# Second layer's codes transposed by DMA, both biases as 32-row tiles on TensorE

## What is computed

```python
def bit_linear(x, w, b):
    scale_x = 127.0 / clip(max(abs(x), axis=-1), 1e-05)
    x_dq = clip(round(x * scale_x), -128, 127) / scale_x
    w_dq = clip(round(w / gamma_w), -1, 1) * gamma_w      # gamma_w = mean(abs(w))
    return einsum('bsd,hd->bsh', x_dq, w_dq) + b
gate = silu(bit_linear(x, gate_w, gate_b))
val = bit_linear(x, val_w, val_b)
return bit_linear(gate * val, out_w, out_b)
```

## Time and profile before

| | |
|---|---|
| median of three runs | 839.48 us |
| profiled execution: its own time | 841.52 us |
| profiled execution: from first to last instruction (span) | 839.7 us |
| mean granted clock of TensorE | 0.970 of full speed |
| busy: TensorE, VectorE, ScalarE, GpSimd | 750.2, 697.7, 534.0, 240.2 us |
| DMA, mean rate over the span | 61 GB/s |

### The profile page before, as it was taken

The page is one execution under the profiler, slowest core; times in us unless marked ns, Lnnn a source line. Parts: engine busy times, 40 slices in busy tenths (PEclk is TensorE's granted clock), DMA queues, the critical chain, the costliest instruction groups (busy, mean ns, idle before and its releaser), DMA issues.

```text
span 839.7 us, 14590 instructions
## 1 busy us (share of the span) xinstructions
PE 750.2 (89%) x4886; PEld 384.6 (46%) x4886; DVE 697.7 (83%) x1412; ACT 534.0 (64%) x693; POOL 240.2 (29%) x427
## 2 busy tenths in 40 slices
PE   4695658969999999999999999999999999999995
PEld 4442344434544454445444544454445444454442
DVE  6778876898889888888988988988888888779982
ACT  4447858767557755784578557855676556745563
POOL 4101003221333324232433333314422332223431
PEclk9898768999999999999999999999999999999998
DMA  8572345101030103011211121111111020001000
GB/s 275 192 261 64 130 165 170 26 14 39 2 95 10 42 26 77 17 37 37 56 37 37 37 52 42 37 37 42 51 37 37 17 52 26 26 2 51 13 26 26
DMA packets 51663, 50.90 MB, mean 61 GB/s; under 512 B 30877, under 2 KB 30877, under 8 KB 50857
## 3 DMA queue, kind: packets, MB, share of 16 engines
q1 hardware_dynamic: 51624, 50.42, 19.2%
HBM read 39.91 MB, written 10.50 MB: 60 GB/s over the span
## 4 chain that ended last, share of the span: by engine, by line
PE 45%; DVE 31%; issue 11%; ACT 10%; POOL 1%; DMA 1%; DVEq 0%; POOLq 0%; ACTq 0%
PE psum L1444 14%; PE psum L1399 13%; PE psum L1435 7%; DVE arena L988 4%; DVE psum L983 3%; ACT arena L749 2%; DVE arena L1088 2%; PE psum L1402 2%; PE psum L1427 2%; PE psum L1378 2%; DVE xmax L1060 1%; DVE arena L1096 1%; PE psum L1470 1%; DVE stats L1048 1%; DVE arena L922 1%
## 5 line engine op out<-in xcount | busy, mean ns | idle before, releaser
L1399 PE MATMUL psum<-ternary,xqT 128*128 128x512 f16 x1024 | 261.3, 379 | 2.8 <-DVE xqT L1009 2.6
L554 POOL TENSOR_TENSOR rstd<-var_e,minus_half 128x1 f32<-128x1 f32 x64 | 40.0, 625 | 406.5 <-DVE var_e L1028 263.9
L1399 PEld LDWEIGHTS psum<-ternary,xqT 128*128 128x128 f16 x1024 | 96.3, 98 | 108.3 <-DVE xqT L1009 3.5
L1435 PE MATMUL psum<-ternary,arena 128*128 128x512 f16 x512 | 128.0, 383 | 1.2 <-ACT arena L726 1.2
L693 ACT ACTIVATE arena<-psum,dequant 128x512 f32<-128x512 f32 x128 | 87.2, 682 | 43.2 <-PE psum L1402 42.8
L983 DVE SCALAR_TENSOR_TENSOR psum<-psum,dequant,valb_b 128x512 f32<-128x512 f32 x128 | 96.3, 752 | 20.2 <-PE psum L1399 19.7
L988 DVE TENSOR_TENSOR arena<-psum,arena 128x512 f32<-128x512 f32 x128 | 88.5, 692 | 20.8 <-ACT arena L693 17.1
L1444 PE MATMUL psum<-wo_hi,arena 128*128 128x512 f16 x256 | 84.4, 392 | 2.5 <-DVE arena L1096 1.9
L1444 PE MATMUL psum<-arena,wq_hi 128*128 128x512 f16 x256 | 77.5, 385 | 7.1 <-ACT arena L740 7.1
L726 ACT ACTIVATE arena<-psum,round_c 128x1024 f16<-128x1024 f16 x64 | 71.3, 1114 | 19.1 <-PE psum L1427 18.7
L701 ACT ACTIVATE arena<-arena,round_c,hscale 128x1024 f32<-128x1024 f32 x64 | 75.9, 1236 | 4.6 <-DVE hscale L1004 4.4
(11 more groups left out here) (181 smaller groups left out, 1348.7 us busy)
## 6 DMA issues: line engine op xcount, KB each, us to landing
arena<-in_x SPq DMA_DIRECT2D x64, 256.0 KB, 2.7
out<-arena SPq DMA_DIRECT2D x32, 256.0 KB, 2.0
arena<-in_L_ffn_gate_w SPq DMA_DIRECT2D x4, 1024.0 KB, 10.0
arena<-in_L_ffn_out_w SPq DMA_DIRECT2D x3, 1024.0 KB, 9.6
ternary<-in_L_ffn_val_w SPq DMA_DIRECT2D x2, 1024.0 KB, 10.2
kcur<-k_scratch SPq DMA_DIRECT2D x64, 32.0 KB, 2.2
ternary<-in_ctx SPq DMA_DIRECT2D x1, 1024.0 KB, 5.4
ternary<-in_L_xattn_Wk SPq DMA_DIRECT2D x1, 1024.0 KB, 8.0
```

What stands on the lines that cost most here:

```text
L1399: ins = M.matmul(ps[:], xqT[:, t % 2, k, :], w[:, k, cols], start=(k == 0), stop=(w is wv and k == KC - 1))
L1435: ins = M.matmul(psO[:], hidT[:, k, :], wo2[:, k, :], start=(k == 0), stop=(k == FC - 1))
```

## The change

The codes of the second layer no longer go through TensorE. Behind the two roundings, `quant` now has two casts: each half of the rounded tile goes, with the rounding constant taken off, into a float16 buffer `hid16`. SP's new `hidden_T` waits for each cast and issues a transposing DMA from that half of `hid16` to `hidT`. `down` waits for both DMAs of its tile. `hidden_transpose`, ScalarE's `hidden_T` and their waits go; a tile's casts wait until the DMAs of the tile before have landed, and the first DMA of a tile for the last down matmul of the tile before. In the first row SP waits once for the last weight transpose.

The value's bias joins the gate's on TensorE: rows 0 to 31 of `bias_parts`, `inv_cols` and `inv_rows` are for the gate, rows 32 to 63 for the value. Both biases are now the first matmuls of a chunk, each with 32 rows, ahead of the eight others; so the gate product's four matmuls now stand behind the wait for psV as well. `hidden` is one pass. `valb_b` and its load go; GpSimd and SP prepare two biases where there was one (six loads of parts instead of three).

```diff
-        bias_left = sb("bias_left", [P, FC])
-        bias_cut = sb("bias_cut", [P, PARTS, FC], BF16)
-        valb_b = sb("valb_b", [P, F])
-
-        unused_abs = valb_b[:, 0:F // 2].bitcast(F16)
+        bias_left = sb("bias_left", [P, 2, FC])
+        bias_cut = sb("bias_cut", [P, 2, PARTS, FC], BF16)
+        hid16 = sb("hid16", [P, F], F16)
+        unused_abs = hid16[:, :]
         unused_abs_last = room(11)[:, 2 * D:].bitcast(F16)
         inv_cols = sb("inv_cols", [P, 2, P], BF16)
         inv_rows = sb("inv_rows", [P, 2, P], BF16)
-        inv = sb("inv", [P, 2])
-        inv_deq = sb("inv_deq", [P, 1])
-        ones_p = sb("ones_p", [P, PARTS])
+        inv = sb("inv", [P, 2, 2])
+        inv_deq = sb("inv_deq", [P, 2])
+        ones_p = sb("ones_p", [P, 2 * PARTS])
...
+            def hidden_T(row, t):
+
+                last, u = ahead(row, t, -1)
+                wait_alone(sp, s_met_sp, o_done, last, u + 1)
+                for h in range(2):
+                    wait_alone(sp, s_met_sp, h16_ready, row, 2 * t + h + 1)
+                    sp.dma_start_transpose(hidT[:, h * FC // 2:(h + 1) * FC // 2, :],
+                                           hid16[:, h * F // 2:(h + 1) * F // 2]).then_inc(hidT_loaded.sem, 16)
+
             def body(b, prev, ffn, att, pre):
                 a, c = b + 1, b + 2
                 for t in range(NT):
                     if pre and (b is not FIRST or t >= 2):
                         normed_x(c, t)
+                    if ffn and not prev and t == 1:
+                        sp.wait_ge(s_wtr, 3 * W_GROUPS)
+                    if prev if t == 0 else ffn:
+                        hidden_T(*ahead(b, t, -1))
...
-                        sp.wait_ge(s_wabs, 3 * W_CHUNKS - 1)
-                        sp.dma_start(valb_b[:, :], bcast(val_b, F)).then_inc(s_vbias, 16)
...
-            sp.wait_ge(s_bst, 16)
-            for i in range(PARTS):
-                sp.dma_start(bias_parts[PARTS * i:PARTS * (i + 1), :],
-                             bias_dram[i:i + 1, :].to_broadcast([PARTS, F])).then_inc(s_brow, 16)
+            sp.wait_ge(s_bst, 16 * 2)
+            for g in range(2):
+                for i in range(PARTS):
+                    row = GROUP * g + PARTS * i
+                    sp.dma_start(bias_parts[row:row + PARTS, :],
+                                 bias_dram[g, i:i + 1, :].to_broadcast([PARTS, F])).then_inc(s_brow, 16)
...
-                whole, left = inv[:, 0:1], inv[:, 1:2]
-                G.tensor_scalar(whole, inv_deq[:], xr[:, t:t + 1], None, ALU.mult).then_inc(iv_ready.sem, 1)
+                whole, left = (inv[:, n, :].rearrange("p (g a) -> p g a", a=1) for n in range(2))
+                cols = inv_cols[:, t % 2, :].rearrange("p (g c) -> p g c", c=GROUP)
+                G.tensor_scalar(inv[:, 0, :], inv_deq[:], xr[:, t:t + 1], None, ALU.mult).then_inc(iv_ready.sem, 1)
                 wait(pool, iv_ready, row, t + 1)
                 for j in range(PARTS):
                     src = left if j else whole
-                    G.tensor_tensor(inv_cols[:, t % 2, j:PARTS * PARTS:PARTS], ones_p[:],
-                                    src.to_broadcast([P, PARTS]), ALU.mult).then_inc(iv_part.sem, 1)
+                    G.tensor_tensor(cols[:, 0:2, j:PARTS * PARTS:PARTS], ones_p[:].rearrange("p (g c) -> p g c", g=2),
+                                    src.to_broadcast([P, 2, PARTS]), ALU.mult).then_inc(iv_part.sem, 1)
...
-                    if n == 0:
-                        last, u = ahead(b, t, -2)
-                        wait(act, hid_tr, last, 2 * u + 2)
...
+                    last, u = ahead(row, t, -1)
+                    wait(act, hidT_loaded, last, 16 * 2 * (u + 1))
+                    for h in range(2):
+                        cols = slice(h * F // 2, (h + 1) * F // 2)
+                        wait(act, hq_ready, row, 2 * t + h + 1)
+                        A.activation(hid16[:, cols], gs[:, t % 2, cols], ACT.Identity,
+                                     bias=round_c[:, 2:3]).then_inc(h16_ready.sem, 1)
...
-                def hidden_T(row, t, h):
-                    wait(act, hid_tr, row, 2 * t + h + 1)
-                    A.activation(hidT[:, h * FC // 2:(h + 1) * FC // 2, :].rearrange("p k n -> p (k n)"),
-                                 half(psO), ACT.Identity, bias=round_c[:, 1:2]).then_inc(hidT_ready.sem, 1)
...
-                    if not prev and (t, n) == (0, 0):
-                        dve.wait_ge(s_vbias, 16)
-                    V.scalar_tensor_tensor(out=psV[n % 2], in0=psV[n % 2], scalar=dequant[:, t, 1:2],
-                                           in1=valb_b[:, n * CW:(n + 1) * CW],
-                                           op0=ALU.mult, op1=ALU.add).then_inc(vb_ready.sem, 1)
-                    wait(dve, vb_ready, b, NCH * t + n + 1)
                     wait(dve, silu_done, b, NCH * t + n + 1)
-                    V.tensor_tensor(part, psV[n % 2], part, ALU.mult).then_inc(hid_ready.sem, 1)
+                    V.scalar_tensor_tensor(out=part, in0=psV[n % 2], scalar=dequant[:, t, 1:2], in1=part,
+                                           op0=ALU.mult, op1=ALU.mult).then_inc(hid_ready.sem, 1)
...
-                    for ps, w, done, used in ((psG[i % 2], wg, g_done, silu_done),
-                                              (psV[i % 2], wv, v_done, hid_ready)):
+                            pe.wait_ge(s_brow, 16 * 2 * PARTS)
+                    for g, (ps, used) in enumerate(((psG[i % 2], silu_done), (psV[i % 2], hid_ready))):
                         if n > 2:
                             wait(pe, used, b, n - 2)
+                        rows_g = slice(GROUP * g, GROUP * (g + 1))
+                        M.matmul(ps[:], inv_rows[rows_g, t % 2, :], bias_parts[rows_g, cols], start=True, stop=False)
+                    for ps, w, done in ((psG[i % 2], wg, g_done), (psV[i % 2], wv, v_done)):
                         for k in range(KC):
-                            ins = M.matmul(ps[:], xqT[:, t % 2, k, :], w[:, k, cols], start=(k == 0),
-                                           stop=(w is wv and k == KC - 1))
-                        if w is wg:
-                            ins = M.matmul(ps[:], inv_rows[:, t % 2, :], bias_parts[:, cols],
-                                           start=False, stop=True)
+                            ins = M.matmul(ps[:], xqT[:, t % 2, k, :], w[:, k, cols], start=False,
+                                           stop=(k == KC - 1))
                         ins.then_inc(done.sem, 1)
...
-                def hidden_transpose(row, t, h):
-
-                    codes = low(gs[:, t % 2, :])
-                    wait(pe, hq_ready, row, 2 * t + h + 1)
-                    if h == 0:
+                def down(row, t, chunks):
+
+                    if 0 in chunks:
                         last, u = ahead(row, t, -1)
                         wait(pe, ys_ready, last, u + 1)
-                    else:
-                        wait(pe, hidT_ready, row, 2 * t + 1)
-                    for i in range(FC // 2):
-                        k = h * FC // 2 + i
-                        ins = M.transpose(half(psO)[:, i * P:(i + 1) * P], codes[:, k * P:(k + 1) * P], eye16[:])
-                    ins.then_inc(hid_tr.sem, 1)
-
-                def down(row, t, chunks):
-
-                    if 0 in chunks:
-                        wait(pe, hidT_ready, row, 2 * t + 2)
+                        wait(pe, hidT_loaded, row, 16 * 2 * (t + 1))
```

More of the change, by code:

```diff
@@ L484, in _ @@
                 sp.dma_start(dst, src).then_inc(s_tab, 16)
-            sp.dma_start(bias_left[:, :], gate_b.rearrange("(p c) -> p c", p=P)).then_inc(s_bias, 16)
+            for g, bias in enumerate((gate_b, val_b)):
+                sp.dma_start(bias_left[:, g, :], bias.rearrange("(p c) -> p c", p=P)).then_inc(s_bias, 16)
             sp.wait_ge(s_bias0, 1)
@@ L792, in body @@
                                 round_w(1, n - 2)
-                        if down and n in (1, 2):
-                            hidden_T(*last, n - 1)
                         if pre and n == 1 and not (b is FIRST and t == 1):
@@ L903, in weight_scale @@
                 V.reciprocal(wrec[:, n:n + 1], wmean[:, n:n + 1]).then_inc(s_wrec, 1)
-                if n == 0:
+                if n < 2:
                     dve.wait_ge(s_wrec, n + 1)
-                    V.tensor_scalar(inv_deq[:], wrec[:, n:n + 1], QMAX, None, ALU.mult)
+                    V.tensor_scalar(inv_deq[:, n:n + 1], wrec[:, n:n + 1], QMAX, None, ALU.mult)
                 then(V.tensor_scalar(deq[:, n:n + 1], wmean[:, n:n + 1], 1.0 / QMAX, None, ALU.mult))
@@ L1562, in body @@
                                 weight_transpose(2, g)
-                        if finish and i in (1, 2):
-                            hidden_transpose(*last, i - 1)
                     if att and t == 1:
```

23 lines of the change are left out of this document (11 added, 12 removed).

## The result

The changed kernel took 857.25 us (median of 4 runs, 855.73 to 857.85) beside 839.63 for the kernel before (4 runs, 838.78 to 840.45): ratio 1.0207, 95% interval 1.0189 to 1.0225. Forecast were 841.8 us, with slower as the likeliest direction and 823 to 885 as the whole range. The time lies 15 us above the value, and 5 us above 852, where the range that the forecast gave its own mechanism ended. The profiled execution has a span of 855.7 us (839.7 before).

A forecast was written before the change was run, and what follows sets the result against it. TensorE was taken to set tiles 0 and 1, all three engines tiles 2 and 3. Start -3, rows +2.3, last row +1, end +2 gave +2.3: 843.8 profiled, 841.8 us as median; range 823 to 885.

The forecast's parts named there:

- own mechanism: Whole kernel: the forecast's main case, 841.8 us with a range of 832 to 852, chance 0.45.
- the serial pair: Rival, each chunk's biases: tiles run one after the other with switches, 0.42 us more per chunk, 863 us; chance 0.10.
- the late DMA: Rival, down product: waits for late transposes, 904 us, chance 0.13; pieces one by one, over 1150, chance 0.05.
- The bias pair: TensorE, each chunk: two 32-row biases beside each other with switches take 0.42 us, 0.20 more than before.
- free switches: Rival, each chunk's biases: pair side by side, switches cost nothing, 0 more per chunk, 826 us; chance 0.27.
- Transposes, passes, casts: Unit prices: 0.45 us per transpose group removed, 0.75 for VectorE's remaining pass, 1.15 for each ScalarE cast.
- Tiles 0 and 1: Tiles 0 and 1 of a full row: bias cost against saved transposes, -0.1 us each.
- The replay of tile 3: Tile 3: casts delay silu(3,0), hidden(3,0), then hidden(3,1); last chunk 1.6 us late; tiles 2 and 3 together +0.5.
- Rows together: Full rows: about +0.35 us each, +2.3 us for 6.5 such rows.
- Start: First row, bound by VectorE: eight saved passes ahead of the scores, -3 us (bounds 0 and -5.5).
- Last row: Last row, no attention, TensorE full: silus 2.3 us late at each edge, +1 us.
- End: End of kernel: last down product waits for casts and DMA (0.35 + 2.7 us), +2 us.

The follow-up runs named there:

- gap_filled: Changed kernel with ten gate matmuls, overwritten afterwards, in TensorE's stop before the last chunk of tile 3 in rows with attention: 846.02 us.
- bias_only: Changed kernel with the codes transposed on TensorE and copied by ScalarE again, the two biases kept as the 32-row pair: 841.98 us.
- late_one_bias: Changed kernel with each tile's casts behind silu 0 and 1 of the next tile, and the value's bias matmul left out: 828.48 us.
- dma_only: Kernel before with only the transposes by DMA and the casts behind the rounding, biases made as before (value's lower half used twice): 860.76 us.
- casts_later: Changed kernel with each tile's two casts moved into the next tile, behind silu 0 and silu 1: 829.05 us.
- hidden30_late: Changed kernel, casts untouched, with VectorE's hidden(3,0) moved behind the statistics of the next tile: 833.79 us.
- no_bias: Changed kernel without the two bias matmuls of each chunk, waits in the same places: 835.82 us.
- before_h30: Kernel before with only VectorE's hidden(3,0) moved behind the statistics: 842.44 us.

## Why the prediction was right in direction and short in size

That the time lies in 823 to 885 is in good part luck. The forecast's own mechanism had 832 to 852, and the upper end of the wide range stood for two rivals, the serial pair and the late DMA, of which neither happened. The direction does not hang on the clock: with the stop filled (gap_filled) the change is still slower, by 5.4 us.

**The bias pair: right.** Forecast 0.42 a chunk; the chunk of 2.15 less eight pitches of 0.217 leaves 0.41, and bias_only shows the 0.84 per tile. The two rivals about it (free switches, 826; a serial pair, 863) are excluded by the 0.10 each way and by late_one_bias. Among my signs I had 0.42 between first bias and first gate matmul; that was misworded, for 0.10 of it lies ahead of the bias, and the distance is 0.32.

**Transposes, passes, casts: right.** 0.45 a group (dma_only, tiles 1 and 0); 0.746 for the pass (0.75); 1.136 for the cast (1.15).

**Tiles 0 and 1: right.** -0.1 each forecast, -0.05 measured.

**The replay of tile 3: right in every link, wrong in what follows it.** The casts delay `silu(3,0)`, VectorE's order carries it to `hidden(3,1)`, TensorE's last chunk waits in its value bias. From the rounding to that bias it gave 495.7 - 484.65 = 11.05 us; the trace has 589.36 - 578.47 = 10.89. But it went on at the pitch of full clock. Forecast for tiles 2 and 3 was +0.5; measured +1.42 (-1.48 and +2.90), of which 1.53 is the clock by gap_filled: without it -0.11. A row came to 89.09 us, not to 88.1. This is the step that failed in the middle of the kernel: the last chunk and the down product behind a stop that the kernel before did not have (its longest in a row, 1.05 us in tile 2, left the clock at 1.00). The sum had no term for this; it was worth 10.5 us in rows 0 to 6.

**Rows together: short.** +2.3 forecast; rows 1 to 6 alone +6.5.

**Start: wrong by 4.** -3 forecast up to row 1, +1.2 measured. casts_later has -2.0 there: the saving of VectorE is real, but row 0 has the same stall in its tile 3, and I had left it out of the sum for the first row.

**Last row: +1 forecast, +4.2 measured.** The tile without attention stops twice, 1.39 and 0.47 us, and its next eight matmuls run mostly at half clock (3.21 instead of 1.83). hidden30_late has the same two stops and keeps the clock:

```profile
804.87 0.38 PE L1402 MATMUL psum<-bias_parts,inv_rows 32*128 32x512 bf16 x1 [1.39 <-ACT arena L703]
...
806.04 1.90 PE L1405 MATMUL psum<-ternary,xqT 128*128 128x512 f16 x8
```

So 1.4 of the 4.2 are the clock and need not come every time. That tile I had priced by its silus alone. Even casts_later is 1.9 behind there; 0.71 us of it is a wait for a DMA, the rest I have not followed up.

**End: +2 forecast, +4.0 measured.** From the last rounding to the down product 8.04 instead of 5.73 us: +2.3, near the forecast, though by other terms: the second DMA leaves 1.3 us behind the first, because one issue takes 1.24 us, and lands 3.2 later, where I had 0.35 and 2.7. Then the sixteen down matmuls last 6.44 instead of 5.22. I had written that the clock costs the same after a longer wait, and the runs don't refute it: behind waits of 8.66 to 8.77 us the sixteen took 5.05 (no_bias), 5.19 (dma_only), 5.35 (gap_filled) and up to 6.44, behind the 1.21 of the old end 5.22 (before), 5.32 (bias_only) and 6.56 (before_h30). So these 1.2 us are scatter of the single execution, not the price of the wait. The last 0.4 lies behind them.

**The late DMA (904, or above 1150): excluded.** Both halves land within some 4.5 us of the first issue (839.67 to 844.22), and TensorE waits for them twice in the whole run, 8.67 us at the end and 1.08 at the first down product of row 0.
The Trainium skill (Advanced Engine Details and Errata, X-Bar Transpose (TRN2)) says that a transposing DMA is as fast as a plain one. By 3.2 us against 2.8 for the plain x tiles of the same 256 KB the trace nearly agrees. The 1.309 us that the Trainium skill gives for one 128x128 block (VectorE: DVE Perf Modes, The three transpose paths) does not add up over the eight blocks of an instruction: that estimate was 10.5, the trace has 3.2.

Counting up: 16.0 us of span, against 2.3. The clock behind the stop of tile 3 is 10.5 (gap_filled against the changed kernel: 1.1 in row 0, 9.4 in rows 1 to 6). The other 5.5 are -2.1 up to the first rounding, +2.3 in row 0, -2.9 in rows 1 to 6, +4.2 in the last row and +4.0 at the end.

## What to carry to other kernels

Where a step is moved to another engine at equal cost, ask what is queued behind it there: 2.2 us of casts per tile, moved from ahead of the first `silu` to behind the first two, were worth 28 us. When a replay of the engines' orders ends in a new stop of TensorE of some 2 us, give the sum a term for the lower clock behind it (here 1.2 to 2.9 us each time), and a range down to nothing. Count each unrolled row and the end by themselves: row 0, the last row and the end held 11.6 us of the difference, against 6.5 in the six rows between.

## What the runs showed of the hardware

- In the changed kernel each of six stops of 2.40 us and one of 1.73 in a busy stream was followed by a stretch at 1.2 GHz: the next sixteen matmuls took 4.70 to 6.31 us instead of 3.46. Ten overwritten matmuls in the stop kept the clock at 2.4 GHz each time and saved 11 us.
- The length of a stop alone does not decide it: stops of 3.07 us left the clock at 1.00 in three rows of no_bias and lowered it in others; two stops of 1.39 and 0.47 us with one matmul between them lowered it in the changed kernel and not in hidden30_late. Stops of 0.53, 0.76 and 1.05 us were followed by full clock in the rows shown.
- Two 32-row tiles in different PSUM banks run side by side: the second costs nothing. In and out of them TensorE loses 0.10 us each.
- A DMA transpose of 128x1024 16-bit values in SBUF lands in 3.2 us, and its issue takes 1.24 us on the queue, where that of a plain load takes 0.35. The DMAs' mean busy share in a row rose from 0.14 to 0.27. The other transfers felt little of it: the x tiles landed in 2.8 us instead of 2.7, and GpSimd waited once for one, 1.1 us; in casts_later they took 3.1 and GpSimd waited seven times, 6.0 us in all.
